# Four score banks in the cross attention of layer 0, with half of its query tiles, output tiles and norms moved out of the attention loop

## The reference

```python
# layer 0: two sets of weights (v_, l_), chosen per token by a type mask
h = rms_norm(x, ln_in_w);           x = x + dense(self_attention(rope(h @ qkv), causal))
h = rms_norm(x, ln_post_cross_w);   q = h @ cq_w                  # 16 heads of 16
k, v = split(ctx @ ckv_w)                                          # 375 keys
p = softmax(q * scale @ k.T)                                       # no mask
x = x + (p @ v) @ cdense_w
h = rms_norm(x, ln_post_attn_w);    x = x + (silu(h @ gate) * (h @ up)) @ down
# layers 1 and 3: layernorm, masked cross attention (16 heads of 64), gated residual, GELU feed forward
# layer 2: memory attention (one head), gate, rms norm
```

## Time and profile before

| | us |
|---|---|
| median of 3 runs | 2069.14 (2064.5 to 2082.28) |
| the profiled execution | 2069.67 |
| its span, first to last instruction | 2067.9 |
| granted TensorE clock, mean | 0.959 |

### The profile page before, as it was taken

One profiled execution on the slowest core, in us unless ns is written; L12 is line 12 of the kernel. 1 busy time (PEld: TensorE's weight loads), 2 busy tenths in 40 slices (PEclk: granted clock), 3 DMA queues, 4 the chain that ended last, 5 costly groups with the idle time before them and its releaser, 6 DMA issues.

```text
span 2067.9 us, 35600 instructions
## 1 busy us (share of the span) xinstructions
PE 1948.2 (94%) x12588; PEld 1665.5 (81%) x12588; DVE 1152.2 (56%) x2919; ACT 838.6 (41%) x2201; POOL 886.1 (43%) x1037
## 2 busy tenths in 40 slices
PE   4999979997999999999999989998979999999998
PEld 3876667776899998988888878995558888887997
DVE  7777857777453454346767644212184667654422
ACT  2026436666221121146666613222234666651321
POOL 3340321232388999951212056860043212103885
PEclk9999977897799999999999999999989999999999
DMA  3110100010133333410000032332121000001332
GB/s 125 41 57 2 47 15 9 19 32 32 42 103 103 111 119 116 125 56 10 18 13 23 2 117 90 105 102 87 61 86 33 18 10 23 13 2 42 102 105 84
DMA packets 38190, 118.87 MB, mean 57 GB/s; under 512 B 6168, under 2 KB 10264, under 8 KB 38016
## 3 DMA queue, kind: packets, MB, share of 16 engines
q1 hardware_dynamic: 31408, 107.92, 16.5%
q10 hardware_dynamic: 6608, 8.68, 1.4%
HBM read 114.75 MB, written 1.84 MB: 56 GB/s over the span
## 4 chain that ended last, share of the span: by engine, by line
PE 81%; DVE 9%; POOL 5%; issue 3%; ACT 2%; DMA 1%; DVEq 0%; SPq 0%; ACTq 0%; POOLq 0%
PE psum L565 15%; PE psum L566 13%; PE psum L567 13%; PE psum L781 7%; PE psum L792 6%; PE psum L835 5%; PE psum L558 4%; PE psum L686 4%; PE psum L688 4%; PE psum L687 4%; POOL wl L1681 3%; DVE rstd L1254 1%; PE psum L849 1%; DVE xc L1269 1%; DVE masked_t L1369 1%
## 5 line engine op out<-in xcount | busy, mean ns | idle before, releaser
L1681 POOL TENSOR_TENSOR wl<-raw,wh 128x256 fp32r<-128x256 f32 x656 | 518.5, 821 | 13.7
L565 PE MATMUL psum<-nh,wh 128*128 128x448 f32 x904 | 347.4, 384 | 14.7 <-DVEq L1456 8.0
L1673 POOL TENSOR_SCALAR wh<-raw 128x1024 fp32r<-128x1024 f32 x164 | 183.9, 1121 | 410.6 <-PE psum L567 170.9
L1039 ACT ACTIVATE probs_t<-masked_t,nmin 112x375 f32<-112x375 f32 (+1 forms) x512 | 279.4, 547 | 163.9 <-DVE nmin L1369 163.8
L566 PE MATMUL psum<-nl,wh 128*128 128x448 f32 x904 | 335.6, 371 | 0.0
L567 PE MATMUL psum<-nh,wl 128*128 128x448 f32 x904 | 335.0, 371 | 0.0
L1369 DVE CUSTOM_DVE_ANT_0 masked_t<-psum,maskf 112x375 f32<-112x375 f32 x384 | 194.7, 545 | 160.3 <-PE psum L781 158.6
L1528 DVE TENSOR_TENSOR hid_l<-scr,hid_h 128x448 fp32r<-128x448 f32 x108 | 95.5, 885 | 229.6 <-ACT hid_h L1120 229.0
L1396 DVE TENSOR_SCALAR probs_t<-probs_t,rinv 112x376 f32<-112x376 f32 (+1 forms) x520 | 213.4, 452 | 9.4
L792 PE MATMUL psum<-cst,probs_t 112*125 112x112 f32 (+1 forms) x1304 | 201.7, 288 | 15.3 <-ACT probsT_t L1062 13.2
L792 PEld LDWEIGHTS psum<-cst,probs_t 112*125 112x125 f32 (+1 forms) x1304 | 179.8, 198 | 41.4 <-issue 15.9
(11 more groups left out here) (189 smaller groups left out, 3734.2 us busy)
## 6 DMA issues: line engine op xcount, KB each, us to landing
raw<-in_walls SPq DMA_DIRECT2D x183, 512.0 KB, 3.5
raw<-in_ctxF SPq DMA_DIRECT2D x24, 375.0 KB, 3.0
ctxb<-in_ctxF ACTq DMA_DIRECT2D x8, 375.0 KB, 3.5
ctxt<-in_ctxK ACTq DMA_DIRECT2D x8, 375.0 KB
x<-in_xT ACTq DMA_DIRECT2D x2, 896.0 KB, 11.1
outT<-x SPq DMA_DIRECT2D x2, 896.0 KB, 5.7
mask<-in_kmask ACTq DMA_DIRECT2D x16, 41.0 KB, 2.6
vself<-in_tt SPq DMA_DIRECT2D x1, 448.0 KB, 6.3
```

Of the source, the lines that this page charges most:

```text
L565: nc.tensor.matmul(out, ah, bh, start=(i == 0), stop=False)
L1039: nc.scalar.activation(probs[s % NPROB][:, 0:a.nk], src, ACT.Exp, scale=-1.0, bias=nmin[:, s % NPROB:s % NPROB + 1], accum_out=rsum[:, s % ...
L1681: last = nc.gpsimd.tensor_tensor(low[cut], src[cut], high[cut].bitcast(F32), ALU.subtract)
```

## The change

- Scores of `att_c0` have four banks: 3, 4, and 1, 2 of the pool. During this attention the pool is bank 0 alone (`plan.use([0])`); behind it, once all exponentials are done, it is banks 0 to 2 again.
- For it, VectorE's minimum is a plain `tensor_reduce` out of PSUM, and Exp reads PSUM. `masked_t` and the tile of zeros are not used there. A score bank is free with its exponentials: the products of a turn wait for those of two turns before.
- `WITHIN` is gone. The whole of `cq` with norm (1,1) stands before the attention, and the whole of `cdense` with norm (2,0) behind it. Both norms use the usual scratch, the former in three parts (squares, root, the rest) between the tiles.
- `WORK` has the chunk of `cdense` behind the last context, and `kv1` no longer waits for norm (2,0).
- In `smallest`, the wait that protects the column of `nmin` (`NPROB` steps back) now stands in every attention; the masked ones keep their own behind it.

```diff
-        [u for b in range(2, B) for u in ((0, "ctx0", b), (0, "mcross", b)) + (tuple(uses("cdense")) if b == 6 else ())] +
-        with_kv1(uses("gu")) +
+        [u for b in range(2, B) for u in ((0, "ctx0", b), (0, "mcross", b))] + uses("cdense") + with_kv1(uses("gu")) +
...
+        self.bank = []
+        self.banks = list(range(POOL))
+        self.last = {}
+
+    def use(self, banks):
+
+        self.banks = list(banks)
 
     def add(self, key, who):
         self.count[who] += 1
+        self.bank.append(self.banks[0])
+        self.banks = self.banks[1:] + self.banks[:1]
...
+        self.s_banks = 4 if mask is None and nh > 1 else 2
...
-            return psum[:, n % POOL, :]
-
-        def s_bank(s):
-            return psum[0:S, 3 + s % 2, :]
+            return psum[:, plan.bank[n], :]
+
+        def s_bank(a, s):
+            return psum[0:S, (3, 4, 1, 2)[s % a.s_banks], :]
...
-            "cq": by_half(2, 2, pieces(1, 1, (0, 1))),
-            "cdense": by_half(4, 4, pieces(2, 0, (0, 3))),
+            "cq": by_half(2, 2, parts(1, 1, s=(0, 0), v=(0, 1), f=(0, 1))),
+            "cdense": by_half(4, 4, parts(2, 0, s=(1, 0), v=(1, 1), f=(1, 1))),
...
-        WITHIN = {1 + i: ("cq", 2 + i) for i in range(11)}
-        WITHIN.update({44 + i: ("cdense", i) for i in range(13)})
...
                 n = plan.add(key, who)
-                if n >= POOL:
-
-                    w, count = plan.order[n - POOL]
+                bank_free(plan.bank[n])
+                plan.last[plan.bank[n]] = n
+                return n
+
+            def bank_free(bank):
+
+                if bank in plan.last:
+                    w, count = plan.order[plan.last[bank]]
                     pe.wait_ge(emptied[w], count)
-                return n
...
-                if s >= 2:
-
-                    pe.wait_ge(a.maxed, s)
+                if s >= a.s_banks:
+
+                    if a is att_c0:
+                        pe.wait_ge(a.exped, s - a.s_banks + 2)
+                    else:
+                        pe.wait_ge(a.maxed, s)
+                elif s >= 2:
+
+                    bank_free(1)
+                    bank_free(2)
...
-                        if a is att_c0 and n in WITHIN:
-                            name, j = WITHIN[n]
-                            (cq if name == "cq" else cdense)(items=[j])
...
-            cq(range(2))
+            stage("cq", nhl, KD, ("dve",), 2, nn=1)
+            plan.use([0])
             attention(att_c0)
-            cdense(range(13, len(SEQ["cdense"])))
+            pe.wait_ge(att_c0.exped, att_c0.steps)
+            plan.use(range(POOL))
+
+            stage("cdense", nhl, KC, ("dve",), 4, ready=lambda half, m: pe.wait_ge(att_c0.out, att_c0.steps // 8))
...
-                        src = s_bank(s)[:, 0:a.nk] if a is att_2 else masked_s[s % NMASK][:, 0:a.nk]
+                        src = s_bank(a, s)[:, 0:a.nk] if a.mask is None else masked_s[s % NMASK][:, 0:a.nk]
...
                 dve.wait_ge(a.scored, s + 1)
+                if s >= NPROB:
+                    dve.wait_ge(a.exped, s - NPROB + 1)
+                if a.mask is None:
+                    nc.vector.tensor_reduce(col, s_bank(a, s)[:, 0:a.nk], AX_X, ALU.min).then_inc(a.maxed, 1)
+                    return
                 if s >= NMASK:
                     dve.wait_ge(a.exped, s - NMASK + 1)
...
                     if name == "kv1":
                         pool.wait_ge(att_c0.scored, att_c0.steps)
-                        norm_done(pool, 2, 0)
```

More of the change, by code:

```diff
@@ L760, in scores @@
                         pe.wait_ge(a.exped, s - 1)
-                    product(s_bank(s)[:, 0:a.nk], [(hw[:, k, bcols(b)], ctxb[:, b % 2, k, 0:S2]) for k in range(KC)])\
+                    product(s_bank(a, s)[:, 0:a.nk], [(hw[:, k, bcols(b)], ctxb[:, b % 2, k, 0:S2]) for k in range(KC)])\
                         .then_inc(a.scored, 1)
                     return
-                if s >= 2:
-                    pe.wait_ge(a.maxed, s)
+                if s >= a.s_banks:
[6 more added lines that the diff above has]
+                    bank_free(2)
                 wide = a.nk + a.nk % 2
@@ L780, in scores @@
                             q, k = (qd, ql)[i][rows, s // 8 % 2, h // 2 % 4, :], keys_of(a, s // 2)[rows, j, :]
-                        last = nc.tensor.matmul(s_bank(t)[:, 0:wide], q, k, start=(n == 0), stop=(n == len(passes) - 1))
+                        last = nc.tensor.matmul(s_bank(a, t)[:, 0:wide], q, k, start=(n == 0), stop=(n == len(passes) - 1))
                         if n == len(passes) - 1:
@@ L898, in dense @@
                       ready=lambda half, m: pe.wait_ge(att_self.out, att_self.steps // 8 * (half + 1)))
-            def cq(items):
-                stage("cq", nhl, KD, ("dve",), 2, nn=1, items=items)
-            def cdense(items):
-                stage("cdense", nhl, KC, ("dve",), 4, items=items,
-                      ready=lambda half, m: pe.wait_ge(att_c0.out, att_c0.steps // 16 * (half + 1)))
             stage("qk", nhl, KD, ("dve", "dve"), 1, nn=0)
@@ L958, in norm_part @@
                 kind, wname, bname, e = NORMS[nn]
-                xc, sq, _, std, _ = scratch(nn, half)
                 if part in S_PART:
@@ L990, in norm_part, with stage @@
                         ins.then_inc(nhigh, 1)
-            def stage(name, each, items=None):
-                for j in items or range(len(SEQ[name])):
-                    it = SEQ[name][j]
+            def stage(name, each):
+                for it in SEQ[name]:
                     if it[0] == "norm":
@@ L1103, in cq @@
                 nc.scalar.mul(qch[:, m, hcols(half)], pool_bank(n)[:, 0:HALF], -0.25).then_inc(q_high, 1)
-            stage("cq", cq, range(2))
+            stage("cq", cq)
             attention(att_c0)
@@ L1108, in _ @@
                 context(att_1, b)
-            stage("cdense", None, range(13, len(SEQ["cdense"])))
+            stage("cdense", None)
             def hidden(name):
@@ L1217, in norm_part @@
                 w = vec[:, VECS.index(wname), :]
-                xc, sq, total, std, rstd = scratch(nn, half)
                 if part == "a":
@@ L1409, in attention @@
                         out_group(a, (w + 1) * a.pair // a.outgroup - 1)
-                    if a is att_c0 and n in WITHIN:
-                        name, j = WITHIN[n]
-                        stage(name, cq if name == "cq" else residual("cdense"), [j])
             for t in (ctxh, ctxl):
@@ L1517, in cq @@
                     .then_inc(emptied["dve"], 1)
-            stage("cq", cq, range(2))
+            stage("cq", cq)
             attention(att_c0)
-            stage("cdense", residual("cdense"), range(13, len(SEQ["cdense"])))
+            stage("cdense", residual("cdense"))
             def hidden(name, gate=None):
```

23 lines of the change are left out of this document (2 added, 21 removed).

## The result

The median is 2064.0 us (20 runs, 2059.4 to 2069.1) against 2070.6 of before (20 runs, 2062.5 to 2082.3) on the same chip: a ratio of 0.9966, 95% interval 0.9952 to 0.9980. The kernel is about 7 us faster, where 11.7 were forecast. The profiled execution took 2059.6 us around a span of 2057.7.

A forecast was written before the change was run, and what follows sets the result against it. Layer-0 cross attention was taken as slowed by work woven into it and by VectorE-set stretches followed by TensorE at 1.2 GHz. 2069.7 - 35.5 + 10.5 + 13.5 = 2058 us, range 2034 to 2074.

The forecast's parts named there:

- Pace of 3.0: Layer-0 cross attention loop: 3.0 us per pair of heads, 189.0 for 63 intervals against 224.5, so -35.5 us.
- Riders: Second half of `cq`, `cdense` and norms woven into the attention loop: taking them out saves 30.5 us.
- Banks: Attention loop: four score banks instead of two save 5 us.
- Grown by as much: Attention loop, sign of being right: idle time for `nmin` gone, that for `probsT_t` before transposes grown by as much.
- One bank: Attention's projection tiles share bank 0: some 0.2 us late, seven times, about 1 us, inside the pace.
- Rival 3: Attention's single projection bank decides: each of 29 tiles waits 1.8 us, 52 us in all; 2115 us, chance 0.04.
- Rival 1: Attention loop: four banks shorten TensorE's idle moments and keep the clock up; pace 2.65, 2036 us, chance 0.29.
- the idle time of the transposes stays: Attention loop, argument against Rival 1: TensorE's wait before the transposes, 10.6 us for `probsT_t`, remains.
- Rival 2: Attention loop: banks bring nothing and the clock falls every cycle; 3.20 us a pair, 2071 us, chance 0.22.
- Head: Before the attention: second half of `cq` and norm (1,1) lose their cover, +10.5 us (9.3 to 11.8).
- Tail: Behind the attention: first half of `cdense` and norm (2,0) delay the MLP, +13.5 us (12 to 15).
- At nothing: VectorE's second wait in other attentions, zero-mask memset, POOL's moved chunk and `kv1`'s dropped wait: all covered, no cost.

The follow-up runs named there:

- early squares: Changed kernel with norm (1,1) started earlier, its squares behind the last dense tile, root and rest ahead of the first query tile: 2054.3 us.

## Why the prediction was right or wrong

- **The sum.** 2058 against 2064.0, inside the range, and within 1% of before as the likeliest case had it. The gain is little more than half of what was forecast (6.6 of 11.7 us). The pace carried it and both ends were priced too low: the scores start at 311.5 instead of near 309, and the MLP's second tile comes 24.75 us behind the first product of `cdense`, outside the 21.5 to 23.5 that were to show the prediction right.
- **Pace of 3.0.** 189.0 forecast, 188.5 measured. Riders: 30.5 forecast, 28.9 shown by two banks with riders out. Banks: 5 forecast, 7.0 shown, of which 4.4 are pace and the rest is one fall of the clock fewer, which the prediction had not asked of the banks. That the sum comes within 0.5 us is in part luck, since single falls of 3.7 us are in both. The choice near the upper end was right, for the reason given: most of the wait came back in front of the transposes.
- **"Grown by as much".** From before to after the transposes' idle time grew from 12.3 (10.6 and 1.7) to 14.7, while the 7.2 for `nmin` went. That comparison has the riders in it. Between the kernels that differ in the banks alone, 9.5 went and 6.0 came back: two thirds moved, one third was gained.
- **Minimum and Exp.** 539 ns against 544, 574 against 601: as forecast.
- **One bank.** Right for the attention's own 29 tiles; no wait of a projection product for it is among the larger ones of after. Rival 3 was priced as if all tiles met it; in the run with riders inside three tiles did, for 5.2 us in all, the longest 3.02.
- **Rival 1, the banks keep the clock up.** It did not come: the mean clock over the pairs is 0.86 (0.84 with two banks and the riders out), with falls near pairs 3, 27, 43, 54 and 59. More banks only moved the idle times; filling them held the clock at 0.96 to 0.98 over 311 to 490, where it had been 0.88 to 0.89. My step "the idle time of the transposes stays" was the one that decided, and it should have cost this rival more of its 0.29. Its pace of 2.65 was too low as well: it was read from seven pairs, and the one of the eight that was left out is a long one (pair 37 takes 3.30 us in after, 414.13 to 417.43). Eight pairs without a fall take 22.27 / 8 = 2.78 with two banks, 21.7 / 8 = 2.71 with four. The Trainium skill, which I had put beside this rival ("TensorE: Matmul & The Clock Gate", section "A second HAM failure mode: psum-queue depth-cycling"), says that frequent short idle times between groups of matmuls make the clock swing. The trace agrees, by the runs in which they were filled. The section says nothing of how many banks keep them away; that four would was my reading.
- **Rival 2, a fall in every cycle.** It did not come either. Some cycles have a fall and others none, and which do differs between kernels with the same loop.
- **Head: 10.5 forecast (to 11.8), 13.1 measured.** The mis-sized terms: the first query copy itself ended 0.7 later; norm 8.2 from its reciprocal on instead of 7.9, since POOL laid out queries beside it (with early squares POOL had nothing to do there and it took 7.9); and what comes behind at half clock. The low products took 1.7 us where 0.5 was set, and the last tile was at half clock nearly to its end, for which both ends had been kept and 2.5 to 5.0 allowed. The sum of squares was complete at 295.65, 0.75 past its step, most of it the later copy. That the head was 5.7 longer than it had to be because of the order of the pieces (early squares) I had not asked.
- **Tail: 13.5 forecast (to 15), 15.3 and 1.3 at half clock measured, 16.6.** Squares and root hit their step: the reciprocal starts at 524.73, which is t + 13.1. The step that failed is the sentence that POOL's part "is covered": its idle 62.25 us showed that its work is never waited for, not that it hurts nobody. It split the next chunk during the norm, and the norm took 9.8 us instead of 7.9. The low products ended 1.8 behind it instead of 0.4, at half clock.
- **At nothing.** Right as far as the trace shows: in layer 1's attention VectorE's minima still wait 58.0 us for score products, in 32 places, as before (57.9), so it has the same room, and the second wait used none that was missed.

## What to carry to other kernels

When work is taken out of a loop to stand by itself, price it without its cover and at the lower clock, in the order in which it will now run, and look at what other engines will do in the same microseconds: an engine that no one waits for can still slow another. An extra buffer in front of a chain takes away the wait that it names, and the next one gives most of it back. Where the clock falls behind short gaps and the gaps can't be removed, a few products that nobody reads, put into the gaps, were worth about as much here as the buffer (5.9 and 8.4 us of the loop, against 7.0). And before a difference of a few us in such a loop is put down to a change, count the falls on both sides: one is worth 3.7 here.

## What the runs showed of the hardware

- **TensorE's clock.** In this loop it falls from 2.4 to 1.2 GHz behind short gaps of TensorE, but not behind each: in after, gaps of 0.39, 0.99 and 0.80 us in front of the transposes at 408.50, 411.07 and 418.99 were followed by no fall, the like gaps of 0.41 and 0.98 at 430.20 and 432.78 by one. A fall costs some 3.7 us here (25.4 against 21.7 for eight pairs). Adding two or three idle products (three take 0.88 us) to each of three turns in eight removed the falls from pairs 6 to 54 in the profiles of three kernels out of three.
- **POOL and VectorE.** VectorE's instructions with two inputs in SBUF took 1.15 us instead of 0.64 (scaling) and 0.62 (low part) while POOL split weights. The reciprocal, with one input, kept its 2.95 us beside POOL (297.56 to 300.51), and additions with an input in PSUM their 0.62 (567.66, while POOL split from 565.65 to 568.85). The Trainium skill, "SBUF — State Buffer", section "Who interferes with whom", says that a VectorE instruction with two SBUF inputs contends with a GpSimd instruction that reads SBUF, and one with at most one such input does not, apart from certain fast modes. The trace agrees in which instructions are hit, and when: POOL's pieces end at 531.68, and the low part at 532.09 and the scaling behind it took their usual 0.61 and 0.67 again. POOL pays as well: its query layouts of 0.84 us took 1.23 to 1.28 from 300.70 on, while VectorE scaled.
- **VectorE's busy time is not its price.** Taking 56.5 us of work off VectorE, which had been busy for 76% of the loop, gave 18 us; of the 16.8 seen in the loop about half was the clock.
